# Expert rows kept by (token, choice): GpSimd scatters them into place, SyncE loads them plainly

## What is computed

```python
x = x + _L0_xattn_ref(_layernorm(x), ctx, ctx)      # 16 heads of 16, no mask
x = x + _L0_ffn_ref(_layernorm(x), gate, w_gate, w_up, w_down)
x = x + _L1_xattn_ref(_layernorm(x), ctx, Wq, Wk, Wv, Wo)   # causal
x = x + _L1_ffn_ref(_layernorm(x), router, w1, b1, w2, b2)

# _L0_ffn_ref: 64 experts, each token goes to its 8 best
topk_w, topk_ids = top_k(softmax(x @ gate.T), 8); topk_w /= topk_w.sum()
h = silu(tokens_of_e @ w_gate[e].T) * (tokens_of_e @ w_up[e].T)
out = h @ w_down[e].T                               # 16,384 rows of 256
y = (unsorted.reshape(tokens, 8, 256) * topk_w[..., None]).sum(axis=1)
```

## Time and profile before

| | us |
|---|---|
| median of 3 runs | 1505.9 |
| the runs | 1501.64, 1505.9, 4754.02 |
| device time of the profiled execution | 1501.42 |
| its span, first to last instruction | 1499.6 |
| TensorE busy (matmuls) | 1007.6, 67% |
| DVE busy | 617.9, 41% |
| GpSimd busy | 483.5, 32% |
| ACT busy | 361.8, 24% |
| mean granted TensorE clock | 0.826 |

### The profile page before, as it was taken

The page is one execution under the profiler, slowest core; times in us unless marked ns, Lnnn a source line. Parts: engine busy times, 40 slices in busy tenths (PEclk is TensorE's granted clock), DMA queues, the critical chain, the costliest instruction groups (busy, mean ns, idle before and its releaser), DMA issues. The chain is left out here.

```text
span 1499.6 us, 26078 instructions
## 1 busy us (share of the span) xinstructions
PE 1007.6 (67%) x5671; PEld 650.4 (43%) x5672; DVE 617.9 (41%) x1846; ACT 361.8 (24%) x884; POOL 483.5 (32%) x641
## 2 busy tenths in 40 slices
PE   5476757640078778888888878601445658859999
PEld 4333434320045555555555555401224436636665
DVE  5467665652023333333333333322535657423220
ACT  4534343410011111111111111110023334512221
POOL 4401334455543333333333333077453320000000
PEclk9868686655589999999999999855567779969999
DMA  6766664100055454445545655235543333210000
GB/s 195 255 172 158 74 74 66 28 18 0 4 154 159 141 165 150 150 150 151 158 147 165 176 164 157 86 98 139 139 112 109 101 99 92 52 69 11 15 14 18
DMA packets 102128, 164.36 MB, mean 110 GB/s; under 512 B 20352, under 2 KB 70400, under 8 KB 101808
## 3 DMA queue, kind: packets, MB, share of 16 engines
q1 hardware_dynamic: 61040, 99.39, 24.4%
q0 software_dynamic: 17984, 43.21, 10.8%
q10 hardware_dynamic: 23040, 20.98, 4.2%
HBM read 174.72 MB, written 45.15 MB: 147 GB/s over the span
## 5 line engine op out<-in xcount | busy, mean ns | idle before, releaser
L1181 PE MATMUL ex_ps<-ex_w_gu,ex_rows_t 128*128 x640 | 278.5, 518 | 89.8 <-DMA ex_w_down<-in_w_down_dram 70.8
L1159 POOL DMA_INDIRECT ex_rows<-moe_rows,ex_idx x160 | 155.5, 972 | 129.1 <-POOL ex_idx L1157 117.7
L835 POOL DMA_INDIRECT expert_lists<-rt_token,rt_idx x128 | 124.4, 972 | 203.9 <-DMA expert_lists<-rt_token,rt_idx 110.4
L647 ACT ACTIVATE a_probs<-a_ps 128x512 f32<-128x512 f32 (+1 forms) x256 | 133.8, 540 | 206.3 <-remote 67.1
L1199 PE MATMUL ex_ps<-ex_w_down,ex_hidden_t 96*128 x640 | 169.6, 388 | 1.0 <-DVE ex_hidden_t L1294 1.0
L492 PE MATMUL a_ps<-stacked_keys,a_qst 96*128 96x256 bf16 (+1 forms) x512 | 119.6, 307 | 73.8 <-DMA stacked_keys<-k_stack 30.4
L1181 PEld LDWEIGHTS ex_ps<-ex_w_gu,ex_rows_t 128*128 128x128 f32 x640 | 108.4, 198 | 121.7 <-issue 116.4
L509 PE MATMUL a_ps<-a_qst,stacked_keys 98*128 98x256 bf16 (+1 forms) x512 | 116.5, 301 | 65.9 <-issue 30.3
L1253 ACT ACTIVATE ex_act_g<-ex_ps 128x192 f32<-128x192 f32 x160 | 52.8, 330 | 440.2 <-PE ex_ps L1181 412.3
L1391 POOL DMA_INDIRECT cb_gathered<-expert_outs,cb_idx x128 | 122.1, 954 | 45.0 <-issue 40.9
L1294 DVE COPY ex_hidden_t<-ex_ps 96x256 f32<-96x256 f32 x160 | 67.3, 420 | 142.7 <-PE ex_ps L1191 126.2
(11 more groups left out here) (200 smaller groups left out, 1405.0 us busy)
## 6 DMA issues: line engine op xcount, KB each, us to landing
ex_w_gu<-in_w_gu_dram SPq DMA_DIRECT2D x160, 384.0 KB
ex_w_down<-in_w_down_dram SPq DMA_DIRECT2D x160, 192.0 KB
expert_outs<-ex_result ACTq DMA_DIRECT2D x160, 128.0 KB
k_stack<-split_parts SPq DMA_DIRECT2D x16, 384.0 KB, 2.6
a_qst<-q_stack SPq DMA_DIRECT2D x32, 192.0 KB
stacked_keys<-k_stack SPq DMA_DIRECT2D x32, 192.0 KB
a_qst<-q_stack SPq DMA_DIRECT2D x32, 128.0 KB
stacked_keys<-k_stack SPq DMA_DIRECT2D x32, 128.0 KB
```

The costliest lines, as they stand in the source:

```text
L647: nc.scalar.activation(probs[:, s, 0:cols], ps[:, 2 + s % 2, 0:cols], ACT.Exp, scale=scale).then_inc(exped, 1)
L835: nc.gpsimd.indirect_dma_start(k.lists, bass.IndirectOffsetOnAxis(ap=self.idx[:, t, s:s + 1], axis=0), self.token[:, t:t + 1], None).then_ ...
L1159: nc.gpsimd.indirect_dma_start(rows[:, j, :], None, k.xn.rearrange("t p d -> (t p) d"), bass.IndirectOffsetOnAxis(ap=idx[:, j:j + 1], axis ...
L1181: last = pe.matmul(ps[:, 2 + j % 2, 0:2 * FF], rows_t[:, j % 2, c * P:(c + 1) * P], w_gu[:, bass.ds(ring, 1), c, :].rearrange("p a n -> p ...
```

## The change

Each of the 16,384 rows that the experts make gets a place of its own in DRAM, number token x 8 + choice. The lists carry these places instead of token numbers (`number`), and DVE gets the token of each by a shift of 3 (`k.ids` from `k.places`). Unused entries of a list hold places behind the real ones (`padding`, `spare`), whose rows are read from a blank tile of `moe_rows`. The first fill of `expert_outs` goes, as do `k.slot` and its computation, and one constant.

In `experts` GpSimd's program is written out instead of looped. It takes its index columns straight from `k.ids` and `k.places`, gathers the rows of tile t, and scatters the result of tile t - 8 into `k.outs` (`place`) ahead of that gather; ACT stores nothing. DVE's buffer is free when the scatter has landed (`placed`).

In `Combine` GpSimd does nothing. The 8 rows of a token lie side by side, so SP loads a batch as two plain DMAs of 128 x 8 KB (`load_rows`): the first two batches ahead of everything, the third after the first stack load, the others at the ends of its steps. SP's loop is one round shorter, with the last rounds written out.

```diff
@@ -469,7 +470,7 @@
 
                 side.sync_first(sp, lambda: load((0, 0)))
 
-                emit(sp, step, last=STEPS // 4 - 1)
+                emit(sp, step, last=STEPS // 4 - 1 - side.lead)
                 side.sync_last(sp)
 
...
@@ -790,13 +783,10 @@
 
     def zero_dram(self, sp):
 
-        sp.wait_ge(self.zero_set, 1)
-        sp.dma_start(self.k.lists.rearrange("(p n) o -> p (n o)", p=P), self.zeros[:]).then_inc(self.zeroed, 16)
-        part = self.zeros[:].bitcast(F32).rearrange("p (t d) -> p t d", d=D)
-        n = LISTS // D
-        rest = self.k.outs[EXPECTED:ETILES].rearrange("(g t) p d -> p g t d", t=n)
-        for g in range((ETILES - EXPECTED) // n):
-            sp.dma_start(rest[:, g], part).then_inc(self.outs_zeroed, 16)
+        sp.wait_ge(self.zero_set, 4)
+        sp.dma_start(self.k.lists[0:EXPERTS * TOK].rearrange("(p n) o -> p (n o)", p=P), self.padding[:]).then_inc(self.zeroed, 16)
+        sp.dma_start(self.k.lists[EXPERTS * TOK:EXPERTS * TOK + SPARE * P].rearrange("(p n) o -> p (n o)", p=P), self.spare[:]).then_inc(self.zeroed, 16)
+        sp.dma_start(self.k.xn[TILES:TILES + 1].rearrange("t p d -> (t p) d"), self.blank[:]).then_inc(self.blanked, 16)
 
     def write(self, sp, i, u):
         sp.wait_ge(self.weights_ready, 2 * i + u + 1)
 
 
     def gpsimd(self, pool):
         nc, k = self.nc, self.k
-        nc.gpsimd.memset(self.zeros[:], 0).then_inc(self.zero_set, 1)
+        nc.gpsimd.iota(self.padding[:], [[0, LISTS // P], [1, P]], base=TOK * TOP_K, channel_multiplier=P).then_inc(self.zero_set, 1)
+        nc.gpsimd.iota(self.spare[:], [[1, SPARE]], base=TOK * TOP_K + P * P, channel_multiplier=SPARE).then_inc(self.zero_set, 1)
+        nc.gpsimd.iota(self.number[:], [[P * TOP_K, TILES], [1, TOP_K]], base=0, channel_multiplier=TOP_K).then_inc(self.zero_set, 1)
+        nc.gpsimd.memset(self.blank[:], 0.0).then_inc(self.zero_set, 1)
         pool.wait_ge(self.c_in, 16 * len(self.constants))
-        pool.wait_ge(self.zeroed, 16)
+        pool.wait_ge(self.zero_set, 4)
+        pool.wait_ge(self.zeroed, 32)
 
         for m in range(BATCH):
             pool.wait_ge(self.slots_ready, m + 1)
@@ -833,7 +827,7 @@
                     if turn:
                         pool.wait_ge(self.scattered[q], 16 * turn)
                     nc.gpsimd.indirect_dma_start(k.lists, bass.IndirectOffsetOnAxis(ap=self.idx[:, t, s:s + 1], axis=0),
-                                                 self.token[:, t:t + 1], None).then_inc(self.scattered[q], 16)
+                                                 self.number[:, t, s:s + 1], None).then_inc(self.scattered[q], 16)
         for q in range(IN_FLIGHT):
             pool.wait_ge(self.scattered[q], 16 * TOP_K * TILES // IN_FLIGHT)
...
@@ -981,22 +972,11 @@
             then(nc.vector.tensor_tensor(below[:, a, 1, :], below[:, a, 0, :], some, ALU.mult))
             then(nc.vector.tensor_tensor(below[:, a, 2, :], below[:, a, 0, :], tiles, ALU.mult))
             then(nc.vector.tensor_reduce(sums[:, a, 0:3], below[:, a], AX.X, ALU.add))
-            then(nc.vector.tensor_scalar(sums[:, a, 0:1], sums[:, a, 0:1], float(E - 1), None, ALU.min))
             then(nc.vector.tensor_tensor(sums[:, a, 1:2], sums[:, a, 1:2], distinct[:], ALU.min))
             then(nc.vector.tensor_tensor(sums[:, a, 3:4], self.tile_no[:, a:a + 1], sums[:, a, 2:3], ALU.subtract))
-            then(nc.vector.tensor_scalar(sums[:, a, 3:4], sums[:, a, 3:4], float(TILES - 1), None, ALU.min))
-            then(nc.vector.tensor_scalar(self.row[:, a:a + 1], sums[:, a, 0:1], float(TILES), None, ALU.mult))
-            nc.vector.tensor_tensor(self.row_i[:, a:a + 1], self.row[:, a:a + 1], sums[:, a, 3:4], ALU.add).then_inc(self.rows_ready, 1)
-
-
-        then(nc.vector.tensor_scalar(self.shift_g[:], starts, -float(P), GEND, ALU.mult, ALU.add))
-        then(nc.vector.tensor_tensor(self.shift_g[:], self.shift_g[:], self.list_end[:], ALU.subtract))
-        then(nc.vector.tensor_tensor(self.place_g[:], self.mask[:], self.shift_g[:].unsqueeze(1).to_broadcast([P, TILES, E]), ALU.mult))
-        then(nc.vector.tensor_tensor(self.place_g[:], self.place_g[:], self.place[:], ALU.add))
-        for t in range(TILES):
-            last = nc.vector.max(self.top_g[:, t, :], self.place_g[:, t, :])
-        then(last)
-        then(nc.vector.tensor_scalar(k.slot[:], self.top_g[:], -1.0, GEND, ALU.mult, ALU.add))
+            then(nc.vector.tensor_scalar(self.row[:, a:a + 1], sums[:, a, 0:1], float(TILES), sums[:, a, 3:4], ALU.mult, ALU.add))
+            then(nc.vector.tensor_scalar(sums[:, a, 0:1], sums[:, a, 0:1], float(E - 1), None, ALU.min))
+            nc.vector.tensor_scalar(self.row_i[:, a:a + 1], self.row[:, a:a + 1], float(LISTS + SPARE - 1), None, ALU.min).then_inc(self.rows_ready, 1)
 
 
         dve.wait_ge(self.turned, 1)
@@ -1010,7 +990,9 @@
         dve.wait_ge(self.ids_in, 32)
         nc.vector.tensor_copy(self.ids_f[:], self.ids_raw[:]).then_inc(self.ids_f_ready, 1)
         dve.wait_ge(self.turned, 2)
-        then(nc.vector.tensor_copy(k.ids[:], self.ps[:, 0:ETABLE]))
+        then(nc.vector.tensor_copy(k.places[:], self.ps[:, 0:ETABLE]))
+        then(nc.vector.tensor_scalar(k.ids[:], k.places[:], 3, None, ALU.logical_shift_right))
+        then(nc.vector.tensor_scalar(k.ids[:], k.ids[:], float(TOK + P - 1), None, ALU.min))
 
 
...
         hidden_turned, hidden_copied, down_ready = sem("hidden_turned"), sem("hidden_copied"), sem("down_ready")
         result_ready = sem("result_ready")
-        out_done = [sem(f"out_done{j}") for j in range(R)]
+        placed = [k.indirect(f"{tag}_placed{j}") for j in range(R)]
         ROUNDS = (end - begin) // R
         table = k.table[:, :, begin:end]
-        ids, outs = k.ids[:, begin:end], k.outs[begin:end]
 
...
@@ -1150,17 +1129,27 @@
 
             @block.gpsimd
             def _(pool):
-                def step(i, j):
-                    t = R * i + j
-                    if not isinstance(i, int):
-                        pass_on(pool, result_ready, t - R + 1, k.passed)
-                    nc.gpsimd.tensor_copy(idx[:, j:j + 1], ids[:, bass.ds(t, 1)]).then_inc(staged, 1)
-                    pass_on(pool, staged, t + 1, k.passed)
-                    nc.gpsimd.indirect_dma_start(rows[:, j, :], None, k.xn.rearrange("t p d -> (t p) d"),
-                                                 bass.IndirectOffsetOnAxis(ap=idx[:, j:j + 1], axis=0)).then_inc(rows_in[j], 16)
+                def gather(t):
+                    if t >= R:
+                        pool.wait_ge(result_ready, t - R + 1)
+                    nc.gpsimd.indirect_dma_start(rows[:, t % R, :], None, k.xn.rearrange("t p d -> (t p) d"),
+                                                 bass.IndirectOffsetOnAxis(ap=k.ids[:, begin + t:begin + t + 1], axis=0)).then_inc(rows_in[t % R], 16)
+
+                def place(t):
+                    pool.wait_ge(result_ready, t + 1)
+                    nc.gpsimd.indirect_dma_start(k.outs, bass.IndirectOffsetOnAxis(ap=k.places[:, begin + t:begin + t + 1], axis=0),
+                                                 result[:, t % R], None).then_inc(placed[t % R], 16)
 
                 with needed(pool):
-                    rounds(pool, step)
+                    for t in range(R):
+                        gather(t)
+                    for t in range(R, end - begin):
+                        place(t - R)
+                        gather(t)
+                    for t in range(end - begin - R, end - begin):
+                        place(t)
+                    for j in range(R):
+                        pool.wait_ge(placed[j], 16 * ROUNDS)
 
             @block.tensor
             def _(pe):
@@ -1252,32 +1241,21 @@
                     wait(act, hidden_ready, t - 1)
                     nc.scalar.activation(act_g[:, j % 2], ps[:, 2 + j % 2, 0:FF], ACT.Silu).then_inc(silu_ready, 1)
 
-                def store(i, j):
-                    t = R * i + j
-                    act.wait_ge(result_ready, t + 1)
-                    act.dma_start(outs[bass.ds(t, 1)].rearrange("t p d -> (t p) d"), result[:, j]).then_inc(out_done[j], 16)
-
-                def step(i, j, first=0, left=R):
+                def step(i, j, left=R):
                     silu(i, j)
                     if left > 2:
                         copy_rows(*((i, j + 2) if j < R - 2 else (i + 1, j + 2 - R)))
...
                     with act.Fori(1, ROUNDS - 1) as i:
                         for j in range(R):
                             step(i, j)
                     for j in range(R):
                         step(ROUNDS - 1, j, left=R - j)
-                    store(ROUNDS - 1, R - 2)
-                    store(ROUNDS - 1, R - 1)
-                    for j in range(R):
-                        act.wait_ge(out_done[j], 16 * ROUNDS)
 
             @block.vector
             def _(dve):
@@ -1298,7 +1276,7 @@
```

(44 more changed lines are left out.)

41 lines of the change are left out of this document (14 added, 27 removed).

## The result

The changed kernel takes **1523.6 us** (median of 4 runs, 1519.5 to 1529.0) against 1508.0 (median of 4; one of them stood at 4754): ratio 1.012, 95% interval 1.007 to 1.017. So it is 1.2% slower, clear of the noise and under the 2% that the prediction set as the line of a change. The forecast was 1404. Its profiled execution has a span of 1523.1 us, before 1499.6. Later runs met chips on which the kernel before takes 1416 to 1423 us; on the one of them where both kernels ran (e9) their ratio is 0.980.

The account below looks back on a forecast made before the run. It took TensorE to bound the experts, and GpSimd's gathers to slow attention 1. Terms -7 + 0 + 5 + 2 - 40 - 64 + 6 = -98 from 1501.4 gave 1404 us; range 1375 to 1475 held about 0.8.

Parts of the forecast that it names:

- TensorE is the bound there.: Experts, 414.5 to 965.0: TensorE, busy 454 of 550.5 us, was taken as what bounds the stage.
- the +5 for 160 more indirect DMAs: Experts: scatters join GpSimd, index copies and ACT's stores go; GpSimd barely keeps up; +5 us, lower bound -20.
- the lag: Attention 1: engines wait long for each other while GpSimd issues gathers in an unbroken row; 25 us of the head's gain.
- The upper bound of +160: Experts: 1.0 us lost for each added indirect DMA, priced from attention 1's steps, where 63.7 us went beside 64 gathers.
- My rival: Experts: the lag moves there, up to 1.0 us per added indirect DMA, 1559 us in all; chance 0.14.
- Head of attention 1, -40: First reduction 49.5 us after the start instead of 89.9: 15 from landing, 25 from the lag; bounds -8 and -42.
- Steps of attention 1, -64 + 6: Four steps lose their gathers, -64 us; six more 2 MB row loads on SP cost +1 each, +6.
- the bound of 30: Attention 1: upper bound, +30 us, on the +6 for SP's six further 2 MB row loads.
- Zero stores, -7: Attention 0: dropping eight 512 KB stores lets GpSimd's scatters start earlier; -7 us, bounds 0 and -9.
- Scatters and tables, 0: List scatters and tables before the experts: 0.9 us more for ids against 1.0 less for the index copy; sum 0.
- End of the experts, +2: Last result to attention 1: a scatter costs more to issue and land than a store; +2 us, bounds +1 and +4.
- exclusive lock of DVE and GpSimd: Experts: skill's shared-port rule, speaking against the +5; by it the rival "GpSimd becomes the bound" would hold, +40, 1444 us.

Follow-up runs that it names:

- e9: The changed kernel itself, unaltered, on chip 7: 1392.7 us against 1420.6 for the kernel before, ratio 0.980.
- e7: The kernel before with room for 8 experts' weights instead of 4, on chip 10: 1422.0 us against 1421.4, ratio 1.002.
- e13: Changed kernel with ACT's plain stores for the experts' scatter, plus a useless 512-byte indirect DMA per tile, on chip 11: 1528.6 us against 1504.9.
- e2: Changed kernel with the experts' scatter going to rows in plain count order instead of the tokens' places, on chip 3: 1512.3 us against 1498.5.
- e1: Changed kernel with ACT's plain stores in tile order and no scatter in the experts, on chip 3: 1402.7 us, ratio 0.936.
- e4: Changed kernel with the index copy and its wait put back between each tile's scatter and gather, on chip 3: 1470.9 us, ratio 0.981.

## Why the prediction was wrong, point by point

**The step that failed: "TensorE is the bound there."** I took a busy share of 454 in 550.5 us for the bound and read TensorE's wait for weights as a matter of shared DMA engines. On that stood the second failed step, the +5 for 160 more indirect DMAs, kept near zero "because here GpSimd never issues more than two in a row after the first eight" and because breaks would end the lag: two in a row, with breaks of 289 us in all, were enough to stall SP, and SP had no time to spare. Had I asked for SP's waits I would have found 5.6 us in 550, and that its issues come every 3.41 us while quick tiles take 2.60. In the quiet case the pace is 2.96 us for a tile that brings no new expert (490.33, 493.29, 496.25 in e9) and 3.57 for one that does (486.76 to 490.33):

```profile
486.76 0.35 SPq L1122 DMA_DIRECT2D ex_w_gu<-in_w_gu_dram  x1
...
490.33 0.09 SPq L1122 DMA_DIRECT2D ex_w_gu<-in_w_gu_dram  x1
...
493.29 0.08 SPq L1122 DMA_DIRECT2D ex_w_gu<-in_w_gu_dram  x1
...
496.25 0.35 SPq L1122 DMA_DIRECT2D ex_w_gu<-in_w_gu_dram  x1
```

64 x 3.57 + 96 x 2.96 = 513 us, nearly all of e9's 523.4. The whole stream of issues there runs from 405.4 to 933.1, with 2.0 us of waiting in it. With no slack, SP passes on every stall. In the changed kernel on the chip of the result the same issues come at these distances, 5.5, 4.3 and 5.6 us:

```profile
485.38 0.02 SPq L1122 DMA_DIRECT2D ex_w_gu<-in_w_gu_dram  x1
...
490.85 0.08 SPq L1122 DMA_DIRECT2D ex_w_gu<-in_w_gu_dram  x1
...
495.12 0.00 SPq L1122 DMA_DIRECT2D ex_w_gu<-in_w_gu_dram  x1
...
500.73 0.09 SPq L1122 DMA_DIRECT2D ex_w_gu<-in_w_gu_dram  x1
```

**Experts, +5: measured +116.5.** "It keeps up, barely" was right of GpSimd; the price came by another engine. The upper bound of +160, 1.0 us for each added indirect DMA, was the right side: 116.5 / 160 = 0.73 us. My rival put the point where the gain is gone at 0.6. I gave it 0.14 on the ground that "a slow tile makes GpSimd wait, and the breaks end the lag"; the breaks are there (289 us of them) and don't end it soon enough. On the quiet chip the term is about -7 (523.4 against e7's 530.0), so the +5 was a fair size for a chip without stalls.

The forecast of 1404 is near e9's 1392.7, but by luck: it was a gain of 98 us on 1501, and e9 gains 28 on 1421. Of the 31 us between the spans of e7 (the kernel before, with the larger ring) and e9, 7 lie ahead of the first result, 7 in the experts, 17 between last result and first reduction and 5.5 between that and the first conversion, and the steps give 5.5 back. Most of what I meant to win in the head and the steps was the lag, and there the kernel before has none.

**The lag itself.** The head shows that I had named the right thing. In the kernel before on the chip of the result, DVE's operations of 0.16 us come 0.70 or 1.40 us apart:

```profile
1032.64 0.16 DVE L85 SCALAR_TENSOR_TENSOR cb_newton<-cb_moments,cb_newton 128x2 f32<-128x2 f32 x1 [1.24 <-DVE cb_newton L83]
1033.35 0.16 DVE L87 SCALAR_TENSOR_TENSOR cb_rstd<-cb_newton,cb_rstd 128x2 f32<-128x2 f32 x1 [0.55 <-DVE cb_newton L85]
1034.74 0.16 DVE L83 SCALAR_TENSOR_TENSOR cb_newton<-cb_rstd 128x2 f32<-128x2 f32 x1 [1.23 <-DVE cb_rstd L87]
```

On e7's chip the same code, beside gathers at the same 1.25 us, has them 0.20 apart:

```profile
1017.61 0.16 DVE L85 SCALAR_TENSOR_TENSOR cb_newton<-cb_moments,cb_newton 128x2 f32<-128x2 f32 x1
1017.80 0.16 DVE L87 SCALAR_TENSOR_TENSOR cb_rstd<-cb_newton,cb_rstd 128x2 f32<-128x2 f32 x1
1018.00 0.16 DVE L83 SCALAR_TENSOR_TENSOR cb_newton<-cb_rstd 128x2 f32<-128x2 f32 x1
```

**Head of attention 1, -40: measured -46.** The loads issued at 1088.6 were used at 1096.5, 7.9 us (forecast 8.0); the chains took 17.9 and 17.8 us (20.5 each), without a lag; first reduction 43.7 us after the start (49.5):

```profile
1096.51 3.95 DVE L1394 TENSOR_TENSOR cb_gathered<-cb_gathered 128x512 f32<-128x512 f32 x6 [20.50 <-DMA cb_gathered<-expert_outs]
1114.45 3.94 DVE L1394 TENSOR_TENSOR cb_gathered<-cb_gathered 128x512 f32<-128x512 f32 x6
1132.26 0.55 DVE L586 TENSOR_REDUCE a_blockmax<-a_ps 128x3 f32<-128x384 f32 x1
```

From first sum to first reduction the kernel before takes 67.2 us on the chip of the result and 39.5 (988.64 to 1028.17) in e7: the lag in the head is 27.7 us (forecast 25).

**Steps of attention 1, -64 + 6: measured -40.** The mechanism was right, one term mis-sized. Odd steps fell from 25 to 27 us to 8.5 to 8.8, as forecast, and the even one of 26.2 to 14.2. Four other even ones didn't stay at 12.7 to 14.1 but took 19.2 to 20.8:

```profile
1163.00:1171.50 8.50, 6.27 (x86) 4.40 (x84) 8.09 (x34) 4.55 (x12) 0.00 (x0) 1.00 1.00 343
1171.50:1191.20 19.70, 13.86 (x132) 10.19 (x132) 11.30 (x25) 6.79 (x16) 0.00 (x0) 0.83 0.34 74
1191.20:1200.00 8.80, 7.45 (x86) 5.37 (x84) 8.23 (x33) 4.63 (x12) 0.00 (x0) 0.81 1.02 334
1200.00:1219.40 19.40, 12.79 (x132) 9.94 (x132) 11.36 (x26) 6.77 (x15) 0.00 (x0) 0.82 0.34 74
```

In the odd step SP issues 2 MB of rows ahead of the stacks, the DMA engines are full (1.00, 343 GB/s), and in the even step TensorE waits for the stacks, in the two shown:

```profile
PE a_ps L493 <- DMA stacked_keys<-k_stack: 4.9, 1, 4.9
...
PE a_ps L493 <- DMA stacked_keys<-k_stack: 6.1, 1, 6.1
```

So the row loads cost some 6 us each time, not 1, about 25 in all; inside the bound of 30. On quiet chips the same steps take 18.1 to 20.0 us beside the gathers (three of them in e7) and 18.0 to 19.7 beside the plain loads (four in e9); all steps take 173.7 us in e7 and 179.2 in e9, so there the plain loads are a small loss.

**The rest.** Zero stores, -7: first result 5.5 us earlier; TensorE's wait at 124 us is gone, the last list scatter starts at 393.4 (forecast 392, before 399.5). Scatters and tables, 0: right. End of the experts, +2: 1.5. The Trainium skill's exclusive lock of DVE and GpSimd (SBUF — State Buffer, "SBUF: two separate sides") still has nothing for it here: gathers took 952 to 982 ns beside the scatters. Its other rule there, that engine ports and DMA ports can't slow each other, doesn't settle what was seen: of SP's long instructions in the changed kernel some 115 are arithmetic, moves and checks on registers, 23 are loads from SBUF.

## What to carry to other kernels

Ask for each engine that only issues DMAs how long it waits, before naming a bound: one that never waits while others wait for its DMAs is the bound, however idle it looks in the table of busy time, and two register loads fewer on it were worth 56 to 72 us here. Indirect DMAs can cost time on engines that have nothing to do with their data; count them, break their row, and put a price on them from the stage where they are dense today. Chips differ: the same two kernels stand at 1.012 on one and 0.980 on another, so run the kernel before beside every experiment.

## What the runs showed of the hardware

While GpSimd issues indirect DMAs close together, instructions of SP with medians of 0.02 to 0.27 us can take 0.70 to 0.73 us (a bounds check in the experts: 18 ns median, 723 longest), gaps of more than 0.3 us stand between others (170 in the experts, 3 in e9), and DVE's operations in the head follow each other in steps of 0.70 or 1.40 instead of 0.20. It doesn't depend on the bytes (512 are enough, e13) and little on where they go (e2). On chip 3 one indirect DMA a tile left 7 long instructions (e1) and two made 75 to 108 (e2 to e4). It was there on the chip of the result, whose number isn't on record, and on chips 3 and 11 (kernel before at 1498 to 1508 us), and absent on chips 7 and 10, and on 8 and 15, where only kernels with the short SP program were recorded (kernel before at 1416 to 1423 on these four). What in the chip makes the difference, and which path the stalled instructions share with GpSimd, no run here tells. Every execution here was recorded by the profiler, so whether the recording has a part in it isn't shown either.

A register load from SBUF took SP 0.27 us, with its bounds and address work 0.6 to 0.8 (the three of e9's first tile start at 403.2, 404.0 and 404.6). The Trainium skill (Runtime: NRT & Kernel Launch, "Instruction fetch mechanics") gives some 200 ns a register for loads of registers from HBM; from SBUF the trace of e9 has medians of 263 to 270.
